# Turning a tile on VectorE and the DMA engines in place of TensorE, in a linear-attention retrieval kernel

## Chip, cores and metric

The kernel runs on one core of a Trainium2 chip. The metric is the device time of one execution in microseconds (us).

## What is computed

The reference is a layer norm followed by two branches that are added to the input. Cut to what matters (x has 8 x 256 rows of 512, G = 8 heads of size 128 are used):

```python
xn  = layernorm(x)
q   = xn @ Wq[used heads].T + bq             # 2048 x 1024
s   = elu(q) + 1
ret = (s @ M) / (s . z + 1e-6)               # per head of 128
out = x + repeat(ret, 4) @ Wo.T + xn @ (w * w_scale) + b
```

## The kernel before, in words

Rows are worked on in T = 16 tiles of 128. A weight matrix P = M . Wo (summed over the four repeats) is made once (`product_P`, eight heads), so that for a tile t the kernel needs q = x W (`product_q`, two halves of 512 columns), the dense branch (`product_dense`), s, the denominators, a = s / den (`make_a`), and a . P (`product_attn`). Every product is done in three passes of `float32r` data (hi.hi, hi.lo, lo.hi; lines 680 to 682), each a 128 x 128 weight load and a matmul of 512 columns: 24 matmuls for q, 12 for dense, 24 for attn.

`product_attn` needs a with the head dimension on the partitions. TensorE turns it: `transpose_a` (line 755) is eight 128 x 128 transposes a tile, into two PSUM banks `aT_ps`. ScalarE copies these to `aT_hi` (`copy_aT_hi`, line 388) and VectorE writes the remainder `aT_lo` (`split_aT_lo`, line 566); both are double buffered by t % 2.

The order on each engine is written out by hand, with semaphores between engines. After a head (tiles 0 to 6 of q and dense, the eight `product_P`), one loop runs t = 7 to 15 (LEAD = 7). In iteration t TensorE does `product_q(t)`, `product_dense(t)`, the mean of t+2, `product_attn(t-7)` and `transpose_a(t-5)`. VectorE does the split of tile t-6, `add_bias` (534), `moments` of t+2 (465 to 473), `make_s` (541), `split_xT_lo` (503), `add_dense` (557), `denominator(t-4)` (546 to 553) and `add_attn(t-7)` (573). ScalarE does the copy of tile t-6, the exponentials (367, 369), `copy_xT_hi` (344), `copy_mean` (329) and `make_a(t-4)` (380, eight instructions). GpSimd does `times_z` (261), `add_b` (268), `rstd_of` (224) and `center` (230). A tail then runs `product_attn` of tiles 9 to 15, with the transposes of 11 to 15 between.

SP issues all loads and stores in one order: in the loop `load_x` (162), `load_xT` (167) and the store of an old tile (210, 213). The repeated adds of Wo are issued from GpSimd (250). s sits in a ring `sbuf_s` of SRING = 7 tiles; a is made in place there. PSUM's eight banks are `q_ps` (2), `dense_ps`, `aT_ps` (2), `attn_ps` (2) and `mean_ps`; in the head q also borrows the `attn_ps` and `aT_ps` banks.

Of the kernel before, what the change touches and what calls it, by code (L numbers as in the profile page):

```python
# [5 lines left out]
F32 = mybir.dt.float32  # L6
F32R = mybir.dt.float32r
BF16 = mybir.dt.bfloat16
I8 = mybir.dt.int8
# [9 lines left out]
def retrieval_and_dense(nc, x_d, xT_d, WqT_d, bq_d, WoT_d, MT_d, z_d, w_d, wscale_d, b_d, out_d):  # L19
# [12 lines left out]
    SRING = 7  # L32
    XRING = 4
    HRING = 4
    BEHIND = 4
    assert P == D and HID == 512 and HALF == 512 and R == 4 and T == 16 and G == 8 and K == 4

    with ExitStack() as ctx:
# [41 lines left out]
        w_i8 = w_words[:].bitcast(I8)  # L80
# [13 lines left out]
        def q_bank(t, h):  # L94
            return ([q_ps, attn_ps, aT_ps][t % 3] if t < LEAD else q_ps)[h]
# [48 lines left out]
        aT_filled = sem("aT_filled")  # L144
# [8 lines left out]
        def halves(h):  # L153
            return slice(h * HALF, (h + 1) * HALF)

# [4 lines left out]
        def _(sp):  # L160
# [17 lines left out]

            load_x(0)
# [10 lines left out]
            sp.dma_start(w_words[:], w_d).then_inc(w_in, 16)  # L190
# [12 lines left out]
            for t in range(5, T):  # L203
                if t >= FIRST_LENT:
                    sp.wait_ge(P_filled, t - FIRST_LENT + 1)
                load_x(t)
                load_xT(t)
                if t >= 10:
                    sp.wait_ge(attn_added, t - 9)
                    sp.dma_start(out_d[t - 10], x[:, t - 10, :]).then_inc(stored, 16)  # L210
            for t in range(T - 10, T - 1):
                sp.wait_ge(attn_added, t + 1)
                sp.dma_start(out_d[t], x[:, t, :]).then_inc(stored, 16)
# [7 lines left out]
        def _(pool):  # L221
# [83 lines left out]
            center(7)  # L305
            add_b(0)
# [9 lines left out]
            for t in range(T - BEHIND, T):  # L316
                times_z(t, 0)
                times_z(t, 1)
                add_b(t - BEHIND + 2)
            for t in range(T - 2, T):  # L320
                add_b(t)

        @block.scalar
        def _(act):
# [58 lines left out]
            def copy_aT_hi(t):  # L383
                for h in range(2):
                    act.wait_ge(aT_filled, 2 * t + h + 1)
                    if t >= 2:
                        act.wait_ge(attn_filled, t - 1)
                    nc.scalar.activation(aT_hi[:, t % 2, h * GH:(h + 1) * GH, :].rearrange("p g r -> p (g r)"),  # L388
                                         aT_ps[h][:], ACT.Copy).then_inc(aT_hi_ready, 1)
# [54 lines left out]
            copy_mean(8)  # L444
            for t in range(LEAD, T):
# [12 lines left out]

        @block.vector
        def _(dve):  # L460
# [76 lines left out]
            def make_s(t, h):  # L537
                dve.wait_ge(exp_ready, 2 * t + h + 1)
                if h == 0 and t >= SRING:
                    dve.wait_ge(aT_filled, 2 * (t - SRING) + 2)  # L540
                nc.vector.scalar_tensor_tensor(sbuf_s[:, t % SRING, halves(h)], q_bank(t, h)[:], 0.0,  # L541
                                               ebuf[:, halves(h)], ALU.max, ALU.add).then_inc(s_ready, 1)
# [16 lines left out]

            def split_aT_lo(t):  # L560
                for h in range(2):
                    dve.wait_ge(aT_hi_ready, 2 * t + h + 1)
                    if t >= 2:
                        dve.wait_ge(attn_filled, t - 1)
                    gs = slice(h * GH, (h + 1) * GH)
                    nc.vector.tensor_tensor(aT_lo[:, t % 2, gs, :].rearrange("p g r -> p (g r)"), aT_ps[h][:],  # L566
                                            aT_hi[:, t % 2, gs, :].rearrange("p g r -> p (g r)").bitcast(F32),
                                            ALU.subtract).then_inc(aT_lo_ready, 1)
# [56 lines left out]
            denominator(1)  # L625
            make_s(4, 0)
# [9 lines left out]
            split_P_lo(1)  # L636
            add_dense(5)
# [4 lines left out]
            split_P_lo(3)  # L642
            split_xT_lo(7)
# [7 lines left out]
            split_P_lo(7)  # L651
            for t in range(LEAD, T):
# [12 lines left out]
            for t in range(T - LEAD, T - 1):  # L665
                split_aT_lo(t + 1)
                if t + 3 < T:
                    denominator(t + 3)
                add_attn(t)
# [8 lines left out]
        def _(pe):  # L678
# [67 lines left out]
            def transpose_a(t):  # L746
                pe.wait_ge(a_ready, t + 1)
                for h in range(2):
                    if t == 0:
                        pe.wait_ge(s_ready, 11 + h)  # L750
                    else:
                        pe.wait_ge(aT_lo_ready, 2 * t - 1 + h)
                    for i in range(GH):
                        g = h * GH + i
                        last = nc.tensor.transpose(aT_ps[h][:, i * P:(i + 1) * P],  # L755
                                                   sbuf_s[:, t % SRING, g * D:(g + 1) * D], ident[:])
                    last.then_inc(aT_filled, 1)

# [14 lines left out]
            for i in range(4):  # L773
                nc.tensor.matmul(aT_ps[i % 2][:], warm_r[:, 0:P], warm_r, start=True, stop=True)
# [65 lines left out]
            transpose_a(0)  # L840
# [3 lines left out]
            transpose_a(1)  # L844
            spread_mean(8)
            for t in range(LEAD, T):
                product_q(t, 0)
                product_q(t, 1)
                product_dense(t)
                if t + 2 < T:  # L850
                    spread_mean(t + 2)
                product_attn(t - LEAD)
                transpose_a(t - LEAD + 2)
            for t in range(T - LEAD, T - 1):
                product_attn(t)
                if t + 2 < T:
                    transpose_a(t + 2)
# [43 lines left out]
```

## Time and profile before

| | |
|---|---|
| median of 3 runs | 260.64 us (260.42 to 262.46) |
| profiled execution, its own time | 262.28 us |
| its span in the trace | 260.5 us |
| TensorE busy, share of the span | 251.3 us, 96% |
| VectorE busy | 154.8 us, 59% |
| ScalarE busy | 121.2 us, 47% |
| GpSimd busy | 103.2 us, 40% |
| mean granted TensorE clock | 0.993 |

Busy time is that in which an engine had an instruction running. A matmul is recorded with its whole passage through the array, so two that follow each other overlap in the records; what one costs the engine is the distance between two starts. The span is what the trace covers; the profiled execution's own time is 1.8 us longer.

### The profile page before, as it was taken

The numbers are of one execution on the slowest core, as the hardware profiler recorded it, in microseconds if no ns is written. First come the engines' busy times: TensorE is split into PE (matmuls) and PEld (weight loads), VectorE is DVE, ScalarE is ACT, GpSimd is POOL, SyncE is SP. The second block draws the span as 40 slices with busy tenths as digits, with TensorE's granted clock in tenths as the row PEclk, the third lists the DMA queues.
The fourth block names the chain that finished last, engine by engine and source line by source line (L and its number), as shares of the span: only waits on it lengthen the run. The fifth ranks groups of instructions, "written<-read, shape, count | busy, mean of one in ns | idle before, by whom it ended". The sixth has DMA issues, their size and how long they took to land.

```text
span 260.5 us, 3387 instructions
## 1 busy us (share of the span) xinstructions
PE 251.3 (96%) x1156; PEld 202.3 (78%) x1156; DVE 154.8 (59%) x262; ACT 121.2 (47%) x276; POOL 103.2 (40%) x96
## 2 busy tenths in 40 slices
PE   7799999899998999999999999999999999999996
PEld 4467777687775888888888888888888888888885
DVE  4558997985677745657384645657364345555321
ACT  2454545666439544534455444534445345555100
POOL 1565665671301770514426070514405055563000
PEclk9799999999999999999999999999999999999999
DMA  6999999996420003030301203010101001111111
GB/s 217 410 401 413 342 216 216 213 209 133 136 81 0 4 0 121 0 123 0 110 13 37 86 0 121 3 40 0 40 3 40 1 1 44 40 40 40 45 50 69
DMA packets 9808, 26.42 MB, mean 101 GB/s; under 512 B 1088, under 2 KB 1344, under 8 KB 8640
## 3 DMA queue, kind: packets, MB, share of 16 engines
q1 hardware_dynamic: 8928, 19.93, 20.9%
q0 software_dynamic: 864, 6.29, 12.0%
q8 instruction: 9, 0.15, 0.2%
q14 instruction: 7, 0.06, 0.1%
HBM read 22.02 MB, written 4.19 MB: 101 GB/s over the span
## 4 chain that ended last, share of the span: by engine, by line
PE 85%; DVE 7%; ACT 2%; DMA 2%; issue 2%; SPq 0%; DVEq 0%
PE attn_ps L682 11%; PE attn_ps L680 11%; PE attn_ps L681 11%; PE q_ps L680 8%; PE q_ps L682 8%; PE q_ps L681 8%; PE aT_ps L755 5%; PE dense_ps L680 5%; PE dense_ps L682 5%; PE dense_ps L681 5%; PE attn_ps L743 2%; DMA s<-in_WqT 2%; DVE wd_lo L520 1%; DVE q_ps L534 1%; DVE stats L465 1%
## 5 line engine op out<-in xcount | busy, mean ns | idle before, releaser
L261 POOL TENSOR_TENSOR e_and_sz<-s,z_b 128x512 f32<-128x512 f32 x32 | 41.8, 1324 | 32.7 <-DVE den L546 32.7
L380 ACT ACTIVATE s<-s,rden 128x128 f32<-128x128 f32 x128 | 39.2, 389 | 30.3 <-DVE rden L553 30.3
L680 PE MATMUL attn_ps<-P_hi,aT_hi 128*128 128x512 f32 (+1 forms) x128 | 50.2, 393 | 0.0
L682 PE MATMUL attn_ps<-P_hi,aT_lo 128*128 128x512 f32 (+1 forms) x128 | 49.2, 385 | 0.0
L681 PE MATMUL attn_ps<-P_lo,aT_hi 128*128 128x512 f32 (+1 forms) x128 | 49.0, 382 | 0.0
L573 DVE TENSOR_TENSOR x<-attn_ps,x 128x512 f32<-128x512 f32 x15 | 10.4, 691 | 46.4 <-PE attn_ps L682 46.4
L680 PE MATMUL q_ps<-WqT_hi,xT_hi 128*128 128x512 f32 x88 | 36.0, 409 | 0.6 <-DVE s L541 0.6
L682 PE MATMUL q_ps<-WqT_hi,xT_lo 128*128 128x512 f32 x88 | 34.4, 391 | 0.0
L681 PE MATMUL q_ps<-WqT_lo,xT_hi 128*128 128x512 f32 x88 | 34.3, 390 | 0.0
L230 POOL TENSOR_TENSOR xT<-xT,mean_b 128x512 f32<-128x512 f32 x14 | 19.4, 1383 | 33.1 <-ACT mean_b L329 33.1
L224 POOL TENSOR_TENSOR rstd<-vareps,neg_half 128x1 f32<-128x1 f32 x16 | 10.0, 626 | 54.8 <-DVE vareps L473 54.8
L534 DVE SCALAR_TENSOR_TENSOR q_ps<-q_ps,rstd,bq_b 128x512 f32<-128x512 f32 x24 | 18.1, 758 | 21.5 <-PE q_ps L682 21.5
L367 ACT ACTIVATE e_and_sz<-q_ps 128x512 f32<-128x512 f32 x24 | 14.3, 597 | 33.8 <-DVE q_ps L534 33.8
L680 PEld LDWEIGHTS attn_ps<-P_hi,aT_hi 128*128 128x128 f32 x128 | 24.1, 188 | 4.9
L682 PEld LDWEIGHTS attn_ps<-P_hi,aT_lo 128*128 128x128 f32 x128 | 24.0, 188 | 4.9
L681 PEld LDWEIGHTS attn_ps<-P_lo,aT_hi 128*128 128x128 f32 x128 | 24.1, 188 | 4.4
L680 PE MATMUL dense_ps<-wd_hi,xT_hi 128*128 128x512 f32 x64 | 25.7, 401 | 0.9 <-DVE x L557 0.9
L388 ACT ACTIVATE aT_hi<-aT_ps 128x512 fp32r<-128x512 f32 x32 | 17.4, 596 | 17.1 <-PE aT_ps L755 17.1
L682 PE MATMUL dense_ps<-wd_hi,xT_lo 128*128 128x512 f32 x64 | 25.0, 390 | 0.0
L681 PE MATMUL dense_ps<-wd_lo,xT_hi 128*128 128x512 f32 x64 | 24.9, 389 | 0.0
L566 DVE TENSOR_TENSOR aT_lo<-aT_ps,aT_hi 128x512 fp32r<-128x512 f32 x32 | 20.6, 686 | 5.2 <-ACT aT_hi L388 5.2
L369 ACT ACTIVATE e_and_sz<-e_and_sz 128x512 f32<-128x512 f32 x32 | 20.2, 633 | 1.0
(93 smaller groups left out, 408.3 us busy)
## 6 DMA issues: line engine op xcount, KB each, us to landing
x<-in_WoT POOLq DMA_DIRECT2D x6, 1024.0 KB, 9.5
x<-in_x SPq DMA_DIRECT2D x16, 256.0 KB, 3.5
xT<-in_xT SPq DMA_DIRECT2D x16, 256.0 KB, 3.9
out<-x SPq DMA_DIRECT2D x15, 256.0 KB, 2.0
x<-in_WoT SPq DMA_DIRECT2D x2, 1024.0 KB, 14.7
s<-in_WqT SPq DMA_DIRECT2D x3, 512.0 KB, 7.3
s<-in_w_scale SPq DMA_DIRECT2D x1, 1024.0 KB, 10.3
s<-in_WqT SPq DMA_DIRECT2D x2, 256.0 KB, 4.3
```

What stands on the lines that cost most here:

```text
L230: nc.gpsimd.tensor_tensor(xT[:, t % XRING, :, :], xT[:, t % XRING, :, :], mean_b[:, t % 2, :].unsqueeze(1).to_broadcast([P, K, P]), ALU.su ...
L261: nc.gpsimd.tensor_tensor(szbuf[:, halves(h)], sbuf_s[:, t % SRING, halves(h)], z_b[:, halves(h)], ALU.mult).then_inc(sz_ready, 1)
L367: nc.scalar.activation(e, q_bank(t, h)[:], ACT.Relu, scale=-1.0).then_inc(qneg_ready, 1)
L369: nc.scalar.activation(e, e, ACT.Exp, scale=-1.0).then_inc(exp_ready, 1)
L380: last = nc.scalar.activation(a_g, a_g, ACT.Copy, scale=rden[:, t % 2, g:g + 1])
L388: nc.scalar.activation(aT_hi[:, t % 2, h * GH:(h + 1) * GH, :].rearrange("p g r -> p (g r)"), aT_ps[h][:], ACT.Copy).then_inc(aT_hi_ready, 1)
L534: nc.vector.scalar_tensor_tensor(q_bank(t, h)[:], q_bank(t, h)[:], rstd[:, t:t + 1], bq_b[:, halves(h)], ALU.mult, ALU.add).then_inc(q_bia ...
L566: nc.vector.tensor_tensor(aT_lo[:, t % 2, gs, :].rearrange("p g r -> p (g r)"), aT_ps[h][:], aT_hi[:, t % 2, gs, :].rearrange("p g r -> p ...
L680: nc.tensor.matmul(out, x_hi, w_hi, start=start, stop=False)
L681: nc.tensor.matmul(out, x_hi, w_lo, start=False, stop=False)
L682: return nc.tensor.matmul(out, x_lo, w_hi, start=False, stop=stop)
L755: last = nc.tensor.transpose(aT_ps[h][:, i * P:(i + 1) * P], sbuf_s[:, t % SRING, g * D:(g + 1) * D], ident[:])
```

## The change

`transpose_a` and the `aT_ps` banks go. In their place VectorE transposes the 32 x 32 blocks of a tile in place in one instruction of 128 x 1024 (`turn_blocks`), and 16 transfers from SBUF to SBUF put block (i, j) of every head at place (j, i) (`spread_blocks`, issued by SP). Each transfer has 32 partitions, and on each of them eight runs of 32 elements (128 bytes): 256 runs, 32 KB. They land in a buffer `aT` for even tiles and in the memory of `MT` for odd ones (free once all eight `product_P` are done). `copy_aT_hi` and `split_aT_lo` now read SBUF. For tiles 12 to 15 SP issues 12 of the 16 transfers and ScalarE the other four (`spread_last_blocks`). BEHIND goes from 4 to 3, so a(t) is made one iteration earlier; SRING goes from 7 to 6; `w_words` shares the memory of `aT`. The two free PSUM banks become a second pair for q, so that `product_q(t)` waits for `make_s(t-2)` in place of t-1.

```diff
-    SRING = 7
+    SRING = 6
-    BEHIND = 4
+    BEHIND = 3
-        q_ps = [bank("q0_ps"), bank("q1_ps")]
-        aT_ps = [bank("aT0_ps"), bank("aT1_ps")]
+        q_ps = [bank(f"q{i}_ps") for i in range(4)]
# SP
+            def spread_blocks(t):
+                sp.wait_ge(a_turned, t + 1)
+                if t == 1:
+                    sp.wait_ge(P_filled, G)
+                elif t >= 2:
+                    sp.wait_ge(aT_lo_ready, 2 * t - 2)
+                a = sbuf_s[:, t % SRING, :].rearrange("p (g d) -> p g d", g=G)
+                for i in range(4 if t < T - BEHIND - 1 else 3):
+                    for j in range(4):
+                        sp.dma_start(aT_place(t)[j * 32:(j + 1) * 32, :, i * 32:(i + 1) * 32],
+                                     a[i * 32:(i + 1) * 32, :, j * 32:(j + 1) * 32]).then_inc(aT_in[t % 2], 16)
+            spread_blocks(0)
+            for t in range(FIRST_LENT, LEAD + 3):
+                sp.wait_ge(P_filled, t - FIRST_LENT + 1)
+                load_x(t)
+                load_xT(t)
+            spread_blocks(1)
+            spread_blocks(2)
+            for t in range(LEAD, T):
+                if t + 3 < T:
+                    sp.wait_ge(P_filled, t + 3 - FIRST_LENT + 1)
+                    load_x(t + 3)
+                    load_xT(t + 3)
+                spread_blocks(t - BEHIND - 1)
+                if t - LEAD >= 1:
+                    store(t - LEAD - 1)
+            for t in range(T - BEHIND - 1, T):
+                spread_blocks(t)
+                store(t - BEHIND - 1)
# GpSimd, head: times_z(3, 0), times_z(3, 1) after center(7)
# ScalarE
             def copy_aT_hi(t):
+                act.wait_ge(aT_in[t % 2], aT_landed(t))
-                    act.wait_ge(aT_filled, 2 * t + h + 1)
+            def spread_last_blocks(t):     # 4 transfers (i = 3) of tiles 12 to 15
+                act.wait_ge(a_turned, t + 1)
+                act.wait_ge(aT_lo_ready, 2 * t - 2)
             for t in range(LEAD, T):
-                copy_aT_hi(t - LEAD + 1)
                 exp_of(t, 0)
                 if t + 1 < T:
                     copy_xT_hi(t + 1)
                 exp_of(t, 1)
+                copy_aT_hi(t - LEAD + 1)
             for t in range(T - LEAD + 1, T):
                 copy_aT_hi(t)
-                if t + 2 < T:
-                    make_a(t + 2)
+                if t + BEHIND < T:
+                    make_a(t + BEHIND)
+                if T - BEHIND - 3 <= t < T - 2:
+                    spread_last_blocks(t + 2)
# VectorE; head: turn_blocks(0), (1), (2) and denominator(3) are added
+            def turn_blocks(t):
+                dve.wait_ge(a_ready, t + 1)
+                nc.vector.transpose(sbuf_s[:, t % SRING, :], sbuf_s[:, t % SRING, :]).then_inc(a_turned, 1)
             for t in range(LEAD, T):
-                split_aT_lo(t - LEAD + 1)
                 add_bias(t, 0)
                 ...
                 add_bias(t, 1)
+                turn_blocks(t - BEHIND - 1)
                 make_s(t, 0)
                 ...
                 make_s(t, 1)
+                split_aT_lo(t - LEAD + 1)
                 add_dense(t)
                 denominator(t - BEHIND)
+                if t == T - 1:
+                    denominator(T - BEHIND)
                 add_attn(t - LEAD)
             for t in range(T - LEAD, T - 1):
                 split_aT_lo(t + 1)
+                if t + BEHIND < T:
+                    turn_blocks(t + BEHIND)
+                if t + BEHIND + 2 < T:
+                    denominator(t + BEHIND + 2)
                 add_attn(t)
# TensorE: transpose_a and its calls are removed
-                pe.wait_ge(s_ready, 2 * (t - 3 if t < LEAD else t - 1) + h + 1)
+                pe.wait_ge(s_ready, 2 * (t - 3 if t < LEAD else t - 2) + h + 1)
```

## Rows read from the trace of the kernel before

**Rows 1.** The page: span, busy time of TensorE, shares of the chain that ended last.

```profile
span 260.5 us, 3387 instructions
...
PE 251.3 (96%) x1156; PEld 202.3 (78%) x1156; DVE 154.8 (59%) x262; ACT 121.2 (47%) x276; POOL 103.2 (40%) x96
...
PE 85%; DVE 7%; ACT 2%; DMA 2%; issue 2%; SPq 0%; DVEq 0%
```

**Rows 2.** Busy time in stretches: us, then each engine, granted clock, DMA share, GB/s.

```profile
112.00:124.00 12.00, 12.00 (x58) 9.95 (x57) 8.26 (x15) 4.94 (x10) 3.07 (x3) 1.00 0.21 68
220.00:240.00 20.00, 20.00 (x105) 16.84 (x104) 10.95 (x19) 11.20 (x33) 11.47 (x10) 1.00 0.10 39
```

**Rows 3.** The chain that ended last, in order of time: start, us, what.

```profile
97.09 0.88 PE aT_ps L755 x8
...
97.96 0.24 PE q_ps L680
98.20 0.23 PE q_ps L681
...
126.38 0.87 PE aT_ps L755 x8
...
141.06 0.87 PE aT_ps L755 x8
...
220.42 0.87 PE aT_ps L755 x8
221.29 0.23 PE attn_ps L680
...
226.52 0.23 PE attn_ps L682
226.75 0.87 PE aT_ps L755 x8
```

**Rows 4.** VectorE's timeline in the head: start, us, what, idle before.

```profile
62.48 0.76 DVE L534 SCALAR_TENSOR_TENSOR aT_ps<-aT_ps,rstd,bq_b 128x512 f32<-128x512 f32 x1 [1.97 <-PE aT_ps L682]
69.84 0.75 DVE L557 SCALAR_TENSOR_TENSOR x<-dense_ps,rstd,x 128x512 f32<-128x512 f32 x1 [1.56 <-PE dense_ps L682]
79.19 1.28 DVE L566 TENSOR_TENSOR aT_lo<-aT_ps,aT_hi 128x512 fp32r<-128x512 f32 x2
```

**Rows 5.** Groups of instructions by line: busy us, mean ns of one, idle before.

```profile
L546 DVE TENSOR_REDUCE den<-e_and_sz 128x8 f32<-128x1024 f32 x16 | 19.3, 1209 | 0.0
L503 DVE TENSOR_TENSOR xT_lo<-xT,xT_hi 128x512 fp32r<-128x512 f32 x15 | 14.2, 944 | 3.9 <-ACT xT_hi L344 3.8
L520 DVE TENSOR_TENSOR wd_lo<-s,wd_hi 128x1024 fp32r<-128x1024 f32 x2 | 3.4, 1762 | 0.0
L573 DVE TENSOR_TENSOR x<-attn_ps,x 128x512 f32<-128x512 f32 x15 | 10.4, 691 | 46.4 <-PE attn_ps L682 46.4
```

**Rows 6.** Timeline of SP's queue: start, us of the issue, what.

```profile
97.84 0.35 SPq L210 DMA_DIRECT2D out<-x  x1
98.23 0.43 SPq L162 DMA_DIRECT2D x<-in_x  x1
98.71 0.46 SPq L167 DMA_DIRECT2D xT<-in_xT  x1
```

**Rows 7.** Busy time in stretches that hold one 256 KB store, and half of one.

```profile
186.00:187.80 1.80, 1.80 (x9) 1.48 (x8) 1.29 (x2) 0.59 (x2) 0.00 (x0) 1.00 0.39 146
256.20:257.00 0.80, 0.80 (x9) 0.80 (x8) 0.00 (x0) 0.00 (x0) 0.00 (x0) 1.00 0.48 164
```

**Rows 8.** DMA issues of the page: count, KB each, median us to landing.

```profile
out<-x SPq DMA_DIRECT2D x15, 256.0 KB, 2.0
```

**Rows 9.** Timelines of ScalarE and VectorE in the tail.

```profile
220.89 1.09 ACT L388 ACTIVATE aT_hi<-aT_ps 128x512 fp32r<-128x512 f32 x2 [0.39 <-PE aT_ps L755]
224.41 2.45 ACT L380 ACTIVATE s<-s,rden 128x128 f32<-128x128 f32 x8 [2.44 <-DVE rden L553]
234.22 1.29 DVE L566 TENSOR_TENSOR aT_lo<-aT_ps,aT_hi 128x512 fp32r<-128x512 f32 x2 [0.38 <-ACT aT_hi L388]
252.18 0.69 DVE L573 TENSOR_TENSOR x<-attn_ps,x 128x512 f32<-128x512 f32 x1 [3.97 <-PE attn_ps L682]
```

More of the change, by code:

```diff
@@ L94, in q_bank @@
         def q_bank(t, h):
-            return ([q_ps, attn_ps, aT_ps][t % 3] if t < LEAD else q_ps)[h]
+            if t < LEAD and t % 3 == 1:
+                return attn_ps[h]
+            return q_ps[2 * (t % 3 == 2 if t < LEAD else t % 2) + h]
         def last_attn_ps(c):
@@ L143, in retrieval_and_dense @@
         dense_added = sem("dense_added")
-        aT_filled = sem("aT_filled")
+        a_turned = sem("a_turned")
+        aT_in = [sem(f"aT_in{i}") for i in range(2)]
         aT_hi_ready = sem("aT_hi_ready")
@@ L202, in _ @@
             sp.dma_start(b_b[:], b_d.unsqueeze(0).to_broadcast([P, HID])).then_inc(b_in, 16)
-            for t in range(5, T):
-                if t >= FIRST_LENT:
-                    sp.wait_ge(P_filled, t - FIRST_LENT + 1)
+            for t in range(5, FIRST_LENT):
                 load_x(t)
                 load_xT(t)
[L208 to L213, printed above, removed]
+            spread_blocks(0)
[16 more added lines that the diff above has]
+                store(t - BEHIND - 1)
+            for t in range(T - BEHIND - 1, T - 1):
+                store(t)
             for c in range(2):
@@ L305, in _ @@
             center(7)
+            times_z(3, 0)
+            times_z(3, 1)
             add_b(0)
@@ L318, in _ @@
                 times_z(t, 1)
-                add_b(t - BEHIND + 2)
-            for t in range(T - 2, T):
+                add_b(t - 3)
+            for t in range(T - 3, T):
                 add_b(t)
@@ L383, in copy_aT_hi @@
             def copy_aT_hi(t):
+                act.wait_ge(aT_in[t % 2], aT_landed(t))
+                if t >= 2:
+                    act.wait_ge(attn_filled, t - 1)
                 for h in range(2):
-                    act.wait_ge(aT_filled, 2 * t + h + 1)
[L386 to L389, printed above, removed]
+                    gs = slice(h * GH, (h + 1) * GH)
+                    nc.scalar.activation(aT_hi[:, t % 2, gs, :], aT_place(t)[:, gs, :], ACT.Copy).then_inc(aT_hi_ready, 1)
+            def spread_last_blocks(t):
+                act.wait_ge(a_turned, t + 1)
+                act.wait_ge(aT_lo_ready, 2 * t - 2)
+                a = sbuf_s[:, t % SRING, :].rearrange("p (g d) -> p g d", g=G)
+                for j in range(4):
+                    act.dma_start(aT_place(t)[j * 32:(j + 1) * 32, :, 96:], a[96:, :, j * 32:(j + 1) * 32]
+                                  ).then_inc(aT_in[t % 2], 16)
             copy_wq_hi(0, 0)
@@ L444, in _ @@
             copy_mean(8)
+            make_a(3)
             for t in range(LEAD, T):
-                copy_aT_hi(t - LEAD + 1)
                 exp_of(t, 0)
@@ L539, in make_s @@
                 if h == 0 and t >= SRING:
-                    dve.wait_ge(aT_filled, 2 * (t - SRING) + 2)
+                    dve.wait_ge(aT_in[(t - SRING) % 2], aT_landed(t - SRING))
                 nc.vector.scalar_tensor_tensor(sbuf_s[:, t % SRING, halves(h)], q_bank(t, h)[:], 0.0,
@@ L642, in _ @@
             split_P_lo(3)
+            denominator(3)
             split_xT_lo(7)
@@ L744, in product_P @@
                                  ).then_inc(P_filled, 1)
[L746 to L757, printed above, removed]
             def product_attn(t):
@@ L773, in _ @@
             for i in range(4):
-                nc.tensor.matmul(aT_ps[i % 2][:], warm_r[:, 0:P], warm_r, start=True, stop=True)
+                nc.tensor.matmul(q_ps[2 + i % 2][:], warm_r[:, 0:P], warm_r, start=True, stop=True)
             pe.wait_ge(consts_set, 3)
```

29 lines of the change are left out of this document (16 added, 13 removed).

## The prediction

> **What bounds the kernel now.** I read the page first. TensorE is busy for 96% of the span and holds 85% of the chain that ended last [rows 1]. A busy TensorE need not be full, so next come the stretches. In the loop and in the tail it is busy without a gap and at the full clock, while VectorE has 3.7 us free in 12 and the DMA engines are 0.1 to 0.2 busy [rows 2]. Then the chain in order of time: in the loop it never leaves TensorE, and its links follow each other at 0.23 us a matmul. From one group of eight transposes to the next are 141.06 - 126.38 = 14.68 us in the loop and 226.75 - 220.42 = 6.33 us in the tail [rows 3]. So from about 83 us on, where the loop begins, the end is set by how much TensorE is given to do, and anything else decides only when it delivers later than TensorE asks.
>
> **What the change takes away.** One `transpose_a` holds TensorE for 0.87 us [rows 3]. Two lie in the head, nine in the loop (tiles 2 to 10), five in the tail (11 to 15). The 14 behind 83 us give 14 x 0.87 = 12.2 us, if TensorE is still fed. A tile then costs 14.68 - 0.87 = 13.8 us in the loop and 5.46 in the tail.
>
> The two in the head I count at nothing. There `product_P` alternates with the P splits on two banks, and VectorE paces it. The change adds to VectorE three turns and `denominator(3)` (1.21 + 0.17 + 0.20, some 1.6 us), while the 1.28 us split of tile 0 [rows 4] stays among the P splits. The turns of tiles 0 and 1 fit in waits of 1.97 and 1.56 us [rows 4]; `denominator(3)` stands before `split_P_lo(4)` with only short waits to absorb it. Against 2 x 0.87 = 1.7 us gained stand about 1.6 us of VectorE. The bounds are 1.7 us of gain and 1.5 us of loss; I take 0.
>
> **What it adds to VectorE.** The block transpose of 128 x 1024 is not in this trace. Nearest are other instructions of VectorE that read 1024 elements: a reduction at 1.21 us, and a subtraction at 1.76 [rows 5]. I take 1.2, since both have one pass over 1024 elements and the reduction has one input as the transpose has; an upper bound is 2 x 1.21 = 2.4 us. In an iteration the order is bias (q half 0 is full at 2.7 us after the iteration's start), moments 1.1, bias (q half 1 at 5.5), turn, make_s, xT split, make_s, aT split, add_dense, denominator. By the durations of the trace the xT split that the next iteration needs at 13.8 us ends near 8.8, so the turn has 5 us of cover, even at 2.4 us. Behind the turn also queue `add_dense`, due 19.2 us after the start and done near 11.6, and the aT split, due at 22 and done near 10.8. VectorE's sum a tile is 10.1 to 11.3 of 13.8 us. Cost: 0. What the trace cannot say is whether SBUF as source makes the aT copies and splits longer; the 0.69 us of an addition from PSUM against a mean of 0.94 of the xT splits [rows 5], which were longer while GpSimd and DMAs were busy, says at most 0.25 us each, which is under the same cover.
>
> Here a rule speaks against the change. TensorE's transposes cost it 0.87 / 8 = 0.11 us each in the stream [rows 3]. The Trainium skill (VectorE: DVE Perf Modes, section Rules for kernel authors) says to transpose 128 x 128 on TensorE where PSUM will do as destination, and keeps VectorE for 32 x 32. By that rule the detour costs more in total, which is true in busy time here (1.2 us and 16 transfers for 0.87 us); it would lose only if the other queues were on the path.
>
> **What it adds to SP.** This is the term that decides. Each tile costs 16 issues. Now an issue of 128 runs takes 0.35 us after a pause and 0.43 to 0.46 behind another, and back to back the starts are 0.48 us apart [rows 6]. Call this distance c. The new transfers have 256 runs of 128 bytes. If issue time does not depend on the runs, c is 0.48; if all of it is proportional to them, c is 0.05 + 2 x 0.43 = 0.91. There is no row for 256 runs. I take 0.50, near the row, because the issue rows hardly differ between transfers and the wait for a preceding one accounts for most of what does.
>
> In the loop SP has 16c + 3 x 0.48 = 9.4 us a tile against 13.8. The period is passed at c = 0.77. Latency is covered as well: `spread_blocks(t-4)` starts in iteration t once the aT split of t-6 is done, near 10.8 us, ends near 19 and lands 2 us later (a store takes 2.0 [rows 8]); `copy_aT_hi` wants it 7.5 us into iteration t+2, thus at 35. Queued behind it on SP are one store, which nobody awaits before the end, and the loads for t+4, which are wanted a whole iteration later. BEHIND = 3 costs nothing for the same reason: `make_a(t-3)` has the denominators at 13.2 and the turn asks 6 us later. The three spreads at the loop's start are the tightest: tile 1 must wait for the last `product_P` (about 82 us), is issued by 90.5, lands at 92.5, and its copy is wanted at about 91 with slack of 10 us to the product. Cost 0.
>
> **The tail** is where 16 transfers meet 5.46 us. SP issues 12 (ScalarE four, 2 us of its 5.5, in the gaps between a 1.09 us copy and a 2.45 us `make_a` [rows 9]). SP has 12c + 0.48 = 6.5 us a tile at c = 0.50, so it falls behind by 1 us a tile for tiles 12 to 15. Its chain: the last iteration starts at 83.4 + 8 x 13.8 = 193.6. There GpSimd and VectorE need until 17.1 us to have the denominators of tile 13, then come `add_attn(8)` 0.7, the split of tile 10 1.3 and the turn of tile 12 1.2, so spread 12 starts at 20.3, thus at 213.9. Four spreads take 48c + 3 x 0.48. Then landing 2.0, half a copy 0.55, half a split 0.65, and from the start of the last product to the end of the span 260.5 - 252.2 = 8.3 us [rows 1, 9]. Sum: 213.9 + 1.4 + 11.5 + 48c = 226.8 + 48c. With c = 0.50 it is 250.8, with 0.48 it is 249.8, both above what TensorE alone would give, 260.5 - 12.2 = 248.3. So the tail gives back 2.5 of the 12.2 us.
>
> **The DMA engines.** A store of 128 packets of 2 KB holds the 16 engines for 0.39 x 1.8 x 16 = 11.2 us, one of 128 packets of 1 KB for 0.48 x 0.8 x 16 = 6.1 us [rows 7]. The difference is 0.040 us a KB, and about 7 ns a packet are left. A packet of 128 bytes is then 12 ns by the straight line; it is at most the 43 ns of a 1 KB packet, if small packets cost a fixed price. An engine gets 256 of them a tile: 3 to 11 us. I take 3, since the line went through both rows. In the loop even 11 + 2.1 of other traffic (three times 11.2 / 16) fit in 13.8; in the tail 11 do not fit in 5.46.
>
> **The sum.** 260.5 - 12.2 + 2.5 = 250.8 of span, 9.7 less than before. The profiled execution's own time was 262.28, the median 260.64; taken from the median this gives 250.9, which I round to 251.
>
> **The rivals.**
> (1) The issue grows with the runs, to c of 0.58 to 0.69. The tail's formula gives 254.6 to 259.9 of span, thus 254.7 to 260.1. For it: twice as many descriptors must be made by something. Against: 0.35 us after a pause holds the fixed work of an issue as well, so the part for each run is less than 0.35 / 128.
> (2) SP is the bound, slower. From c = 0.69 on the whole chain of spreads decides: 82.3 (last `product_P`) + 11 x 16c + 48c + 6 pairs of loads and 11 stores (11.0) + 11.5 = 104.8 + 224c; it passes 260.5 at 0.695, and gives 284 at c = 0.80 and 309 at 0.91. ScalarE would then wait for `aT_in`, and with it the exponentials, `make_s` and in the end `product_q`.
> (3) Packets of 128 bytes cost as much as 1 KB ones. The tail's pace is then 11 us a tile: 213.9 + 44 + 2 + 11.5 = 271 us. For it: nothing under 1 KB of data stands in the trace. Against: the straight line through two sizes, which leaves 7 ns a packet. The Trainium skill (DMA: Bandwidth & Descriptors, section Specifications) says that below 512 bytes the engines read, modify and write; that would be on this side. The same page (section Bandwidth) holds that transfers between SBUF and SBUF are spared the price of small descriptors, and no run here shows either yet.
> (4) The change does not get its gain for another reason: a wait in the head or a late `x` load. `load_x(10)` stands behind spreads 1 and 2, ends near 101 us and is wanted at 100.7. Some 1 to 3 us, 252 to 254.
>
> **How the numbers follow.** Forecast with (4): 0.53, thus 251. Rival (1) 0.18, half of it below 258.0. Rivals (2) and (3) 0.16 and 0.10, to which I add 0.03 for slower by several small terms. Low end: 248.3 of span with the head's 1.7 gained is 246.6. High end: to leave out no more than 0.2, it takes in rival (3) at 271. A measurement of this kernel cannot tell less than about 1% (2.6 us) from no change. Faster by over 1%: 0.53 + 0.09 = 0.62, and less 0.02 for a head worse than its bound, 0.60. Within 1%: 0.11. Slower: 0.29.
>
> **What would show it.** Right: SP's issues of `spread_blocks` 0.48 to 0.52 us apart; 60 matmuls a tile at 13.8 us; no wait of TensorE in the loop; waits of TensorE for the aT split, under 3 us in total, in the last three or four tiles; a turn at 1.2 us; VectorE's busy time up by some 19 us. Wrong: SP's issues over 0.6 us; ScalarE waiting for the transfers in the loop; a DMA share over 0.5 in the loop; TensorE's gaps before the loop begins, which would show that the head was mis-sized.

## The result, and the profile after

The changed kernel takes 267.51 us (median of 4 runs, 266.14 to 268.63) against 261.55 for the kernel before on the same chip (4 runs, 260.42 to 262.5): ratio 1.0213, 95% interval 1.0145 to 1.028. It is slower by 2.1%, with 1.5 to 2.8% as the interval. The four executions of the changed kernel have spans of 264.3 to 266.8 us, so a span below is compared to about 1 us, and a time inside one trace more closely. The profiled execution took 268.2 us, with a span of 266.4, where the forecast had 250.8. So 15.6 us are to be explained.

The page of the changed kernel: span, busy times, the chain that ended last by engine, then its largest lines; it answers to [rows 1].

```profile
span 266.4 us, 3393 instructions
...
PE 242.3 (91%) x1028; PEld 190.7 (72%) x1028; DVE 179.7 (67%) x278; ACT 120.2 (45%) x276; POOL 105.0 (39%) x96
...
PE 53%; SPq 24%; DVE 12%; issue 4%; DMA 4%; ACT 3%; DVEq 0%
SPq L197 22%; PE q_ps L742 7%; PE q_ps L744 7%; PE q_ps L743 7%; PE attn_ps L742 6%; PE attn_ps L744 6%; PE attn_ps L743 6%; PE dense_ps L742 4%; PE dense_ps L743 4%; PE dense_ps L744 4%; DMA s<-in_WqT 2%; PE attn_ps L805 2%; DVE stats L515 1%; DVE aT_lo L620 1%; DMA x<-in_x 1%
```

TensorE's 85% of the chain have become 53%, and SP's queue, which held 0%, now has 24%, nearly all of it at line 197, the transfers of `spread_blocks`. Next, the waits of TensorE: total, times, longest.

```profile
PE attn_ps L742 <- DVE aT_lo L620: 9.2, 5, 3.0
PE mean_ps L752 <- DVE meanvar L519: 4.0, 3, 3.3
PE dense_ps L742 <- DVE x L607: 3.1, 1, 3.1
```

Each names VectorE, but the cause behind each is another one. For the first, SP's queue shows it: start, us of a whole group of issues, and what. It answers to [rows 6].

```profile
84.22 10.95 SPq L197 DMA_DIRECT2D MT<-s  x16
95.27 10.73 SPq L197 DMA_DIRECT2D aT<-s  x16
106.05 0.60 SPq L171 DMA_DIRECT2D x<-in_x  x1
106.69 0.43 SPq L176 DMA_DIRECT2D xT<-in_xT  x1
...
220.65 7.81 SPq L197 DMA_DIRECT2D aT<-s  x12
228.50 0.60 SPq L202 DMA_DIRECT2D out<-x  x1
229.19 7.87 SPq L197 DMA_DIRECT2D MT<-s  x12
237.11 0.61 SPq L202 DMA_DIRECT2D out<-x  x1
237.82 7.94 SPq L197 DMA_DIRECT2D aT<-s  x12
245.80 0.60 SPq L202 DMA_DIRECT2D out<-x  x1
246.50 8.56 SPq L197 DMA_DIRECT2D MT<-s  x12
```

In the tail one tile follows another at 229.19 - 220.65 = 8.5 us and 246.50 - 237.82 = 8.7, with no pause between groups, while TensorE has 5.46 us of work for each. Twelve issues take 7.81 us, 0.65 each. That is what paces the waits for `aT_lo`. The first two of the five (1.36 and 1.23 us) have a share of ScalarE's: its copy of the tile began right behind its own four issues (219.90 to 222.86, and 228.25 to 230.86). From the third on (1.75, 2.96, 1.85) the copy waited for the transfers themselves. Where the first wait ends, VectorE's split also took 1.74 us beside GpSimd's work, for 0.69 as a rule.

The second wait is at the start of the loop. VectorE's timeline (start, us, what, idle before), and the stretches around it (as in [rows 2]):

```profile
103.06 0.75 DVE L584 SCALAR_TENSOR_TENSOR q_ps<-q_ps,rstd,bq_b 128x512 f32<-128x512 f32 x1
109.15 0.69 DVE L515 BATCH_NORM_STATS2 stats<-x 128x6 f32<-128x512 f32 x1 [5.34 <-DMA x<-in_x]
```

```profile
106.00:108.00 2.00, 0.82 (x4) 0.36 (x2) 0.00 (x0) 0.73 (x2) 0.00 (x1) 1.00 0.54 60
108.00:110.00 2.00, 0.00 (x0) 0.00 (x0) 0.81 (x2) 0.00 (x0) 0.00 (x0) 0.91 0.90 282
110.00:112.00 2.00, 1.88 (x5) 1.59 (x6) 1.97 (x5) 1.02 (x2) 0.55 (x1) 0.50 0.31 50
112.00:114.00 2.00, 2.00 (x8) 1.52 (x8) 2.00 (x5) 1.41 (x4) 0.51 (x1) 0.73 0.31 50
...
118.00:202.00 84.00, 84.00 (x373) 69.20 (x373) 60.83 (x95) 42.13 (x103) 35.43 (x31) 1.00 0.41 92
```

`load_x(10)` is issued at 106.05, behind 32 transfers. `moments(10)` waits for it 5.34 us, the mean product waits for the moments, and TensorE stands for 3.3 us. Then its granted clock is 0.50 (the 1.2 GHz level) for 2 us and 0.73 for 2 more, which costs another 1.0 + 0.54 us: 4.8 in all. The last row is the rest of the loop but its last iteration: TensorE is busy without a gap at the full clock, as forecast.

The third is in the head, in VectorE's timeline:

```profile
44.03 1.21 DVE L596 TENSOR_REDUCE den<-e_and_sz 128x8 f32<-128x1024 f32 x1
45.27 2.04 DVE L599 TENSOR_SCALAR den_e<-den 128x8 f32<-128x8 f32 x1
...
47.46 0.70 DVE L607 SCALAR_TENSOR_TENSOR x<-dense_ps,rstd,x 128x512 f32<-128x512 f32 x1
```

The addition of 128 x 8 takes 2.04 us where it usually takes 0.17, and `add_dense(2)`, for which TensorE waits, stands behind it. GpSimd's timeline has three instructions back to back over the same time:

```profile
43.97 1.57 POOL L267 TENSOR_TENSOR xT<-xT,mean_b 128x512 f32<-128x512 f32 x1
45.22 0.82 POOL L261 TENSOR_TENSOR rstd<-vareps,neg_half 128x1 f32<-128x1 f32 x1
45.76 1.52 POOL L298 TENSOR_TENSOR e_and_sz<-s,z_b 128x512 f32<-128x512 f32 x1
```

The addition ends at 47.31, as the last of them does (47.28). TensorE's granted clock falls behind this stop too, as it did at tile 10 (the third number from the end is the granted clock):

```profile
48.00:50.00 2.00, 1.78 (x4) 1.49 (x5) 2.00 (x5) 2.00 (x7) 0.99 (x2) 0.55 1.15 242
50.00:52.00 2.00, 2.00 (x7) 1.53 (x6) 0.62 (x2) 0.03 (x1) 1.22 (x1) 0.59 0.92 177
```

Those are another 0.9 + 0.8 us of TensorE's time. How much of this reaches the loop's start, the experiments show.

### The profile page after: what moved, and what is told of

Same layout as the page of the kernel before. It is cut to its first block, busy times and chain, and to the rows that moved or that the text cites. A ratio compares the mean times of both kernels' runs of the same rounds, so it can differ in the third digit from the quotient of the medians.

```text
span 266.4 us, 3393 instructions
## 1 busy us (share of the span) xinstructions
PE 242.3 (91%) x1028; PEld 190.7 (72%) x1028; DVE 179.7 (67%) x278; ACT 120.2 (45%) x276; POOL 105.0 (39%) x96
## 3 DMA queue, kind: packets, MB, share of 16 engines
q0 software_dynamic: 864, 6.29, 11.5%
## 4 chain that ended last, share of the span: by engine, by line
PE 53%; SPq 24%; DVE 12%; issue 4%; DMA 4%; ACT 3%; DVEq 0%
SPq L197 22%; PE q_ps L742 7%; PE q_ps L744 7%; PE q_ps L743 7%; PE attn_ps L742 6%; PE attn_ps L744 6%; PE attn_ps L743 6%; PE dense_ps L742 4%; PE dense_ps L743 4%; PE dense_ps L744 4%; DMA s<-in_WqT 2%; PE attn_ps L805 2%; DVE stats L515 1%; DVE aT_lo L620 1%; DMA x<-in_x 1%
## 5 line engine op out<-in xcount | busy, mean ns | idle before, releaser
L742 PE MATMUL q_ps<-WqT_hi,xT_hi 128*128 128x512 f32 x104 | 41.8, 402 | 0.9 <-DVE s L591 0.6
L744 PE MATMUL q_ps<-WqT_hi,xT_lo 128*128 128x512 f32 x104 | 40.6, 390 | 0.0
L743 PE MATMUL q_ps<-WqT_lo,xT_hi 128*128 128x512 f32 x104 | 40.5, 390 | 0.0
L584 DVE SCALAR_TENSOR_TENSOR q_ps<-q_ps,rstd,bq_b 128x512 f32<-128x512 f32 x28 | 21.1, 756 | 25.1 <-PE q_ps L744 25.0
L742 PEld LDWEIGHTS attn_ps<-P_hi,aT_hi 128*128 128x128 f32 x128 | 24.9, 194 | 16.3 <-issue 8.9
L406 ACT ACTIVATE e_and_sz<-q_ps 128x512 f32<-128x512 f32 x28 | 16.6, 594 | 21.8 <-DVE q_ps L584 21.8
L744 PE MATMUL dense_ps<-wd_hi,xT_lo 128*128 128x512 f32 x64 | 25.4, 397 | 0.0
L620 DVE TENSOR_TENSOR aT_lo<-MT,aT_hi 128x512 fp32r<-128x512 f32 x16 | 15.8, 1027 | 13.5 <-ACT aT_hi L428 13.5
L591 DVE SCALAR_TENSOR_TENSOR s<-q_ps,e_and_sz 128x512 f32<-128x512 f32 x28 | 18.7, 674 | 7.6 <-DMA MT<-s 4.3
L742 PEld LDWEIGHTS q_ps<-WqT_hi,xT_hi 128*128 128x128 f32 x104 | 19.5, 188 | 6.0 <-issue 1.2
L743 PEld LDWEIGHTS q_ps<-WqT_lo,xT_hi 128*128 128x128 f32 x104 | 19.5, 188 | 4.4 <-issue 0.5
L744 PEld LDWEIGHTS q_ps<-WqT_hi,xT_lo 128*128 128x128 f32 x104 | 19.5, 188 | 4.2
```

Of the source, the lines that this page charges most:

```text
L406: nc.scalar.activation(e, q_bank(t, h)[:], ACT.Relu, scale=-1.0).then_inc(qneg_ready, 1)
L584: nc.vector.scalar_tensor_tensor(q_bank(t, h)[:], q_bank(t, h)[:], rstd[:, t:t + 1], bq_b[:, halves(h)], ALU.mult, ALU.add).then_inc(q_bia ...
L620: nc.vector.tensor_tensor(aT_lo[:, t % 2, gs, :], aT_place(t)[:, gs, :], aT_hi[:, t % 2, gs, :].bitcast(F32), ALU.subtract).then_inc(aT_lo ...
L742: nc.tensor.matmul(out, x_hi, w_hi, start=start, stop=False)
L743: nc.tensor.matmul(out, x_hi, w_lo, start=False, stop=False)
L744: return nc.tensor.matmul(out, x_lo, w_hi, start=False, stop=stop)
```

## The experiments

All edits are to the changed kernel unless another is named, and `...` marks lines left out. Ratios are to the kernel before, timed on the same chip. "Spread 12" is the start of the first group of 12 transfers in SP's queue, where the tail's chain begins (220.65 in the changed kernel); "loop start" is the first product of q for tile 7 (83.05 before, 84.66 after).

**Is it the queue's order that stops the loop?** `load_x(10)` and `load_x(11)` go ahead of the spreads of tiles 1 and 2, later loads one iteration earlier.

```diff
-            for t in range(FIRST_LENT, LEAD + 3):
+            for t in range(FIRST_LENT, LEAD + 5):
...
-                if t + 3 < T:
+                if LEAD < t and t + 4 < T:
...
```

> The changed kernel with the loads of tiles 10 and 11 issued by SP ahead of the spreads of tiles 1 and 2, and later loads one iteration earlier. Theory A (SP's order and its issue time make the loss): VectorE's wait of 5.3 us for tile 10's x goes, and TensorE's gap of 3.1 us near 107 us and the half clock behind it with it; the last iteration starts 4 to 5 us earlier, so do the spreads of the tail, span 261 to 262.5. Theory B (the spreads are late at the tail for their own sake, SP busy without pause from 84 us on): the start of spread 12 stays near 220 us and the span at 265 to 266.

Measured: 264.52 us (4 runs, 262.2 and 262.7, 266.4 and 266.6: too far apart for a ratio). The profiled one is of the faster pair, span 260.9, 5.5 less; so the size is read inside the trace. The stretches of this kernel, where the changed one stood still:

```profile
106.00:108.00 2.00, 2.00 (x11) 1.61 (x10) 1.23 (x3) 1.97 (x5) 0.17 (x1) 1.00 0.30 49
108.00:110.00 2.00, 2.00 (x10) 1.63 (x9) 2.00 (x3) 0.72 (x3) 1.20 (x1) 1.00 0.30 49
```

Spread 12 comes at 215.39, 5.3 earlier, of which 0.4 was there at the loop start. So the queue's order cost 4.9 us between the loop's start and spread 12, which is the stop and the slow stretch behind it (4.8). The tail's pace is unchanged (215.39, 223.92, 232.58, 241.26).

**Is it `denominator(3)` that makes the head late?**

```diff
-            denominator(3)
             ...
             split_P_lo(7)
+            denominator(3)
```

> The changed kernel with denominator(3) behind the last P split on VectorE instead of ahead of the fifth. Theory A (the head's 1.8 us are those 1.6 us of VectorE in the chain of P): the loop starts 1.5 us earlier, near 83.4 us; the end gains up to 1.5 us, or nothing if the stall for tile 10's x swallows it. Theory B (the head is late because of something else, an odd long instruction near 45 us in that trace): the loop's start moves by less than 0.5 us apart from what that instruction costs.

Measured: 266.75 us (265.15 to 268.95), ratio 1.016 (1.0079 to 1.0241), not told apart from the changed kernel. The profiled execution is the fastest of the four, span 263.4. There the loop starts 3.8 us earlier (80.90), but most of that is not the edit's. The held-up addition fell elsewhere in this trace, in `denominator(1)`, TensorE's wait for `add_dense` is 1.2 instead of 3.1, and its clock stays at 1.00 behind it. The loop starts of the traces, sorted by which addition was held up and by where `denominator(3)` stands, part the two (the others are from experiments below):

| held up | `denominator(3)` as changed | `denominator(3)` late |
|---|---|---|
| `denominator(0)`, ahead of `add_dense(2)` | 84.66; 84.29 (loads first), 84.17 (half the runs), 84.26 (tail by TensorE), 84.77 (128 partitions) | 84.13 (three edits) |
| `denominator(1)` | 81.90 (four transfers) | 80.90 (this kernel), 80.91 (three edits, two inputs) |
| none | 82.88 (one run) | |

So the move is worth 0.0 to 0.6 us in the first row and 1.0 in the second, and the hold-up ahead of `add_dense(2)` 2.3 to 3.2. These are single traces, and the last row shows that about 1 us between two of them needs no such cause. The stop for tile 10's x is still there (TensorE stands for 3.6 us): spread 12 at 217.37, the end 3.0 earlier.

**Does the issue grow with the runs?** Only heads 0 to 3 are moved (ScalarE's four transfers likewise): half the runs and bytes. The turned values of the other heads are left out.

```diff
-  sp.dma_start(aT_place(t)[j * 32:(j + 1) * 32, :, i * 32:(i + 1) * 32],
-               a[i * 32:(i + 1) * 32, :, j * 32:(j + 1) * 32])
+  sp.dma_start(aT_place(t)[j * 32:(j + 1) * 32, 0:4, i * 32:(i + 1) * 32],
+               a[i * 32:(i + 1) * 32, 0:4, j * 32:(j + 1) * 32])
```

> The transfers carry only heads 0 to 3 (the turned values of heads 4 to 7 are left out): 16 transfers of 128 runs in place of 256, in the same two-dimensional form. If the issue grows with the runs, it falls from 0.61 to about 0.43 us and the starts to 0.48 us apart, the tail's SP chain from 8.6 to 6.3 us a tile, and the span to 252 to 255. If the two-dimensional form makes the issue long, it stays at 0.61 us and the span at 265 to 266.

Measured: 268.19 us (266.03 to 268.65), ratio 1.0193 (1.0121 to 1.0264), span 266.8. SP's queue:

```profile
107.41 10.24 SPq L197 DMA_DIRECT2D MT<-s  x16
...
221.88 7.69 SPq L197 DMA_DIRECT2D aT<-s  x12
```

10.24 us for 16 against 10.39 with twice the runs: 0.01 us of an issue hangs on 128 runs. Rival (1) had the size of the issue right and its reason wrong.

**What is the change worth when issues cost nothing?** From tile 2 on only the four transfers with i = j are made (one of them by ScalarE for tiles 12 to 15, and what the copies wait for is lowered to match); the other twelve blocks are left out.

```diff
-                    for j in range(4):
+                    for j in range(4) if t < 2 else range(i, i + 1):
```

> From tile 2 on only the four diagonal transfers of a tile are issued (the other twelve blocks are left out), each with its 256 runs. SP is off the path. Theory A: the removed transposes then show their worth, the tail runs at 5.5 us a tile; the head's 1.8 us and what spread 1 does to the first iteration stay, span 250 to 252. Theory B (something besides SP's issue holds TensorE, as VectorE's extra work or slower reads from SBUF): span 256 or more.

Measured: 248.13 us (247.48 to 252.18), ratio 0.9437 (0.9372 to 0.9502), span 246.6, 13.9 less than before. TensorE has no wait for `aT_lo` and none for the x of tile 10. The chain's shares, and SP's queue:

```profile
PE 82%; DVE 10%; ACT 3%; issue 2%; DMA 2%; SPq 1%; DVEq 0%
```

```profile
107.15 2.55 SPq L197 DMA_DIRECT2D aT<-s  x4
121.02 2.55 SPq L197 DMA_DIRECT2D MT<-s  x4
134.78 2.55 SPq L197 DMA_DIRECT2D aT<-s  x4
148.53 2.55 SPq L197 DMA_DIRECT2D MT<-s  x4
```

The starts follow each other at 13.75 us, the period that the prediction worked out. Of the 13.9 us, 1.15 are an earlier loop start (81.90) and 12.75 lie behind it, for 12.2 forecast there. So with the issues out of the way TensorE's gain comes in full.

**The tail alone.** Tiles 12 to 15 go by TensorE as before, into the second pair of q banks; the other twelve stay as changed.

```diff
+        aT_ps = q_ps[2:]
+        ON_PE = T - BEHIND - 1
-            for t in range(T - BEHIND - 1, T):
-                spread_blocks(t)
-                store(t - BEHIND - 1)
...
+                if ON_PE <= t + 2 < T:
+                    transpose_a(t + 2)
```

> The changed kernel, but tiles 12 to 15 are turned by TensorE as before (into the second pair of q banks, free by then). Theory A (in the tail SP's issue is the pace): the tail goes from 8.6 to 5.5 + 0.9 us a tile, and the gaps of TensorE after 230 us go. By the starts of the changed kernel: loop 84.9, plus 5.4 us of the stall for tile 10's x, plus 9 x 13.8, 6 x 5.46, 4 x 0.87 and 8.3 at the end, 259 us of span. Theory B (TensorE waits in the tail for slower copies and splits whatever turns the tiles): no more than 2 us gained, 264 or more.

Measured: 260.55 us (258.86 to 261.69), ratio 0.9895 (0.9817 to 0.9973), span 259.4. The waits for `aT_lo` are gone, the other two stay:

```profile
PE mean_ps L760 <- DVE meanvar L523: 4.6, 3, 3.8
PE dense_ps L750 <- DVE x L611: 3.2, 1, 3.2
```

The span is 7.0 us shorter, although TensorE has 4 x 0.87 = 3.5 us more to do: the queueing in the tail (SP's, and ScalarE's part of it) cost three times what the change saved there.

**All three edits together.** The loads first, `denominator(3)` later, the tail by TensorE.

> Three edits together: the loads of tiles 10 and 11 ahead of the first spreads, denominator(3) behind the P splits, tiles 12 to 15 turned by TensorE. If the three places are all there is: 83.4 + 9 x 13.8 + 6 x 5.46 + 4 x 0.87 + 8.3 = 252.2 us of span, faster than before by 3%. If an instruction of VectorE again sits blocked for 2 to 3 us in the head, 254 to 256.

Measured: 254.44 us (6 runs, 251.42 to 255.65), ratio 0.9648 (0.9578 to 0.9718), span 252.5. Of the three waits one is left, 3.0 us for `add_dense`, behind an addition of 1.99 us at 45.17.

**What makes the issue long?** Two forms of the 16 transfers, 32 KB each as before, ScalarE's four likewise; data lands in wrong places, so a . P is made of elements in another order. First 32 partitions with one run of 1 KB:

```diff
-  aT_place(t)[j * 32:(j + 1) * 32, :, i * 32:(i + 1) * 32], a[i * 32:(i + 1) * 32, :, j * 32:(j + 1) * 32]
+  aT_place(t)[j * 32:(j + 1) * 32, 2 * i:2 * i + 2, :],     a[i * 32:(i + 1) * 32, 2 * j:2 * j + 2, :]
```

> The same 16 transfers of 32 KB a tile from 32 to 32 partitions, but each partition's 1 KB in one run instead of eight (the blocks go to wrong places; the turning is left out). If the second dimension of the pattern makes the issue long, it falls from 0.61 to 0.43 us. If it is the 32 partitions, or a source in SBUF, it stays at 0.61.

Measured: one run, 264.62 us, span 262.8. The issues of its SP queue:

```profile
104.95 10.02 SPq L197 DMA_DIRECT2D MT<-s  x16
115.01 0.59 SPq L171 DMA_DIRECT2D x<-in_x  x1
115.65 0.43 SPq L176 DMA_DIRECT2D xT<-in_xT  x1
```

Then all 128 partitions with one run of 256 bytes, the partitions of a load but between SBUF and SBUF:

```diff
+  aT_place(t)[:, 2 * i + j // 2, 64 * (j % 2):64 * (j % 2) + 64], a[:, 2 * i + j // 2, 64 * (j % 2):64 * (j % 2) + 64]
```

> The 16 transfers of a tile still go from SBUF to SBUF with 32 KB each, but every one has 128 partitions with one run of 256 bytes (the values land in wrong places; the turning is left out). If the 32 partitions make the issue long, it falls from 0.58 to 0.43 us. If a source in SBUF does, it stays near 0.6, and then every transfer inside SBUF costs SP 0.17 us more than one from HBM.

Measured: one run, 268.19 us, span 266.4.

```profile
107.00 10.13 SPq L197 DMA_DIRECT2D MT<-s  x16
117.18 0.59 SPq L171 DMA_DIRECT2D x<-in_x  x1
117.82 0.43 SPq L176 DMA_DIRECT2D xT<-in_xT  x1
```

Neither runs nor partitions matter: 10.02, 10.13, 10.24 and 10.39 us for 16, with 32 to 256 runs. What all four share and the loads (0.43) do not is that both ends are in SBUF. They are also smaller (16 or 32 KB). Size made no difference between 16 and 32 KB here, nor in the head of the kernel before between loads of 256 and 1024 KB (0.43 each), but no small transfer from HBM was run. So the two ends are what is left by exclusion, not what was shown. The first load or store behind such a group also takes 0.58 to 0.61, which an explanation by the two ends alone does not cover; what the queue does there stays open.

**Does the head gain from TensorE too?** The three edits, and tiles 0 and 1 turned by TensorE as before, with their turns, spreads 0 and 1 and the places in SP's queue taken out.

```diff
-            return t >= ON_PE
+            return t < 2 or t >= ON_PE
```

> As the kernel with the three edits, and tiles 0 and 1 turned by TensorE too (no transfer before tile 2). Two transposes cost 1.7 us in the head, but VectorE loses two turns there, and make_s(7) no longer waits for tile 1 to land. If those waits touch TensorE, 251 to 253 of span, as good as or better than with three edits; if not, 1 to 2 us more than there, 253 to 254.

Measured: 255.43 us (6 runs, 252.32 to 258.46), ratio 0.9671 (0.9601 to 0.9741), span 250.5. By the intervals, no difference from the three edits: turning the first two tiles costs or gives nothing that can be told.

**Is it the form of the blocked addition?** It is written with two inputs, in the kernel with the three edits, in that of the head by TensorE, and in the kernel before.

```diff
-                nc.vector.tensor_scalar_add(den_e[:], den[:], DEN_EPS)
+                nc.vector.scalar_tensor_tensor(den_e[:], den[:], DEN_EPS, den[:], ALU.add, ALU.max)
```

> The kernel with the three edits, and the small addition of the denominators (128x8, one input in SBUF) written with two inputs, (den + eps) max den, the same values. In all traces of changed kernels but one, this instruction once took 2.0 to 3.5 us in place of 0.17 in the head, beside GpSimd's work, and TensorE waited and fell to half its clock. Theory A (the one-input form is kept out for as long as GpSimd has work back to back): the two-input form never takes over 1.5 us, the span falls by 2 to 4 us to 249 to 250.5, and the runs scatter less. Theory B (any instruction of VectorE at that place is kept out): it takes 2 to 3 us as before and the span stays at 252 to 253.

> The kernel in which also tiles 0 and 1 are turned by TensorE, with the same small edit. Theory A: 2 to 3 us less than without it where the addition was kept out, 248 to 250 us of span, runs within 2 us instead of 6. Theory B: as without, 250 to 256.

> The kernel before, with the same small edit of the denominators. Its eleven runs so far lie at 260.3 to 264.9 us. Theory A: its slower runs are those in which the addition is kept out, so all runs come near 260.5 us. Theory B: no change, 260 to 265.

Measured: 253.59 us (6 runs, 251.15 to 256.44), ratio 0.9655 (0.959 to 0.9721); 253.23 (6 runs, 252.26 to 254.93), ratio 0.968 (0.9633 to 0.9728); the kernel before with it, 262.77 (12 runs), ratio 1.0012 (0.9972 to 1.0051). VectorE's timeline of the first of these:

```profile
54.13 3.67 DVE L603 SCALAR_TENSOR_TENSOR den_e<-den 128x8 f32<-128x8 f32 x1
```

The form is not the reason: this one was held up for 3.67 us, and that of the head by TensorE for 2.11.

**Take `add_dense` out from behind the addition.**

```diff
-            denominator(0)
             add_dense(2)
+            denominator(0)
```

> The changed kernel with add_dense(2) ahead of denominator(0) on VectorE. In its trace the small addition of denominator(0) sat for 2.04 us behind GpSimd's work and kept add_dense(2) from TensorE, which waited 3.1 us and then ran at half its clock for some 3 us. Theory A (that is part of the head's loss): the wait for add_dense in the head goes, the loop starts 2 to 4 us earlier, 262 to 264 us of span if it isn't swallowed by the stall for tile 10's x. Theory B (that stall and VectorE's chain of P set the loop's start anyway): within 1 us of 266.

Measured: 264.10 us (12 runs, 263.24 to 266.91), ratio 1.008 (1.0034 to 1.0126), span 265.1. The profiled execution is the slowest of the twelve. The wait for `add_dense` is gone, and the loop starts at 82.37, 2.3 us earlier. The held-up addition is now that of `denominator(1)` (55.35, 3.29 us), behind which TensorE does not wait. The stop for tile 10's x returns most of it: spread 12 is only 1.4 us earlier.

**All four edits together.**

> The kernel with the three edits and the same swap. Theory A: its profiled run goes from 252.5 to 249 to 250.5 us of span and its median from 254.4 to 251 to 252. Theory B: the addition is kept out at another place of the head instead (denominator(1), as in two other traces) and the median stays at 253 to 254.5.

Measured: 250.49 us (6 runs, 248.82 to 252.09), ratio 0.9523 (0.9462 to 0.9585), span 248.7, granted clock 1.0. The page's busy times and chain, and VectorE's timeline:

```profile
PE 238.6 (96%) x1060; PEld 191.0 (77%) x1060; DVE 178.3 (72%) x274; ACT 119.8 (48%) x276; POOL 104.7 (42%) x96
...
PE 86%; DVE 6%; ACT 2%; DMA 2%; issue 2%; SPq 0%; DVEq 0%
```

```profile
44.02 0.74 DVE L611 SCALAR_TENSOR_TENSOR x<-dense_ps,rstd,x 128x512 f32<-128x512 f32 x1
...
53.14 4.53 DVE L603 TENSOR_SCALAR den_e<-den 128x8 f32<-128x8 f32 x1
```

and TensorE's, a little later:

```profile
59.74 1.10 PE L813 MATMUL attn_ps<-x,MT 128*128 128x512 f32 x2 [0.84 <-DVE s L595]
```

The chain is TensorE's again, as it was before the change, and the loop starts at 80.36. This version beats both kernels, 4.8% under the kernel before. An addition is held up for 4.53 us; `make_s` stands behind it, and TensorE waits 0.84 us for that, instead of 3 us and a slow stretch. Whether the kernel before would gain from the same swap was not run; its waits for `add_dense` are only 0.9 us in all.

## Why the prediction was wrong, by its steps

**The tail, the largest part.** The step that failed is "I take 0.50": the terms 48c and 1.4 gave four spreads 25.4 us. From 220.65 to 255.06 they took 34.4, 9.0 more: 48 x 0.15 = 7.2 because the issues start 0.65 apart, 0.8 because each of the three stores between takes up 0.74 instead of 0.48, and 1.0 more, most of it in the last group (8.56). The row taken as nearest was of loads from HBM, and the text even named the only thing it doubted, the runs; what made the issue long was not them (10.02 us for 16 issues with 32 runs, 10.39 with 256). That it is the two ends in SBUF is left by exclusion. The mechanism and the formula were right, but for ScalarE, whose four issues took 2.6 to 3.0 us for 2 forecast and stood ahead of its copy. With c = 0.65 it gives 226.8 + 31.2 = 258.0, inside rival (1)'s span; the rest of the miss lies ahead of the tail.

**The loop's start, the second part.** Spread 12 began at 220.65 instead of 213.9, 6.75 later, of which 1.3 are the head's. (83.4 + 8 x 13.8 is 193.8 and not 193.6, so the sum should have said 214.1.) The step is the loop's "Cost 0" for SP and, in rival (4), "Some 1 to 3 us". The queue order was seen, with `load_x(10)` behind spreads 1 and 2, but its size rested on the same c: 32 issues at 0.65 take 21 us instead of 16, so that the load was issued at 106.05. Moving the load brought 4.9 us. That TensorE would come back at a lower clock (0.50 and 0.73 in the two stretches behind) after 3.3 us of standing was not in the sum; it is 1.5 of these 4.9.

**The head.** Taken as 0 within -1.7 to +1.5. The loop began at 84.66, 1.3 us later than the 83.4 used, and 1.6 later than in the kernel before (83.05), so just outside the bounds. And the step's reason, `denominator(3)` against two transposes, was the smaller part. By the table of loop starts `denominator(3)` cost 0 to 1 us (2.0 between the two kernels with `add_dense` moved, 82.37 and 80.36, the first of them at half the clock from 82 to 84). The hold-up of an addition ahead of `add_dense(2)`, which the prediction did not know, cost 2.3 to 3.2; against it stands what the head gained. The sum of the miss: 9.0 + 6.75 - 0.2 (the end behind the last spread, 11.3 instead of 11.5) = 15.6.

**What held.** TensorE's side: 13.75 us a tile in the kernel with four transfers, and 13.9 us of span gained there against 12.2 + 1.7 forecast as the most. That the two are equal is partly luck: 12.75 came behind the loop's start for 12.2, and 1.15 ahead of it for 1.7. The turn: 1.232 us (mean of 16) for 1.2 forecast. The landing of the transfers: 1.9 for 2.0. The small packets: between 219 and 221 us, 816 packets of 128 bytes took 30.3% of 16 engines' time, as the DMA view of that stretch has it:

```profile
DMA packets 816, 0.10 MB, mean 49 GB/s; under 512 B 816, under 2 KB 816, under 8 KB 816
...
q1 hardware_dynamic: 816, 0.10, 30.3%
```

0.303 x 2 us x 16 / 816 = 11.9 ns each, as the straight line said (12); rival (3) is out. (Its own price was read too low: 6.1 us over 128 packets is 48 ns and not 43. And its sum counts the landing twice, once in the 11.5.) Of the two sections of the Trainium skill set side by side in the prediction (DMA: Bandwidth & Descriptors), the trace agrees with Bandwidth, that transfers between SBUF and SBUF are spared the penalty of small descriptors, and not with Specifications' read-modify-write below 512 bytes, as far as time goes.

The splits became longer at the mean, 1.03 and 0.94 us a half (16 each, from `MT` and `aT`) for 0.69, which is up to 0.34 each and over the bound of 0.25. But SBUF as source is not enough for it: the median is 0.69 as before, the last two, with GpSimd done, took 1.30 us together, and single ones beside GpSimd's work up to 1.78. It stayed under cover in the loop; in the tail one such split ended TensorE's first wait. VectorE's busy time rose by 24.9 us for 19 forecast: 19.7 are the turns, the rest mostly these splits and the hold-up. The DMA share in the loop was 0.41. Rival (2), SP as the bound of the whole loop, did not come: 16c + 1.5 = 12 us is under 13.8, yet c = 0.65 is close to the 0.695 at which that chain alone would have reached the old span.

The range of 246.6 to 271.0 held the time only because it took in rival (3), whose mechanism was not the one at work. That is luck.

## What to carry to other kernels

Before moving work to the DMA queues, count the issues by the issuing engine, take the price of one from a row of the same kind of transfer (both ends in SBUF here: starts 0.65 us apart, not 0.48), and compare groups of them with the period of every stage, the shortest above all: 12 issues at 0.65 us do not fit in 5.5 us, though 16 fit in 13.8. A load that stands behind such a group is as late as the whole group; put it ahead. A mixed solution, with the detour where the period is long and the old way where it is short, and with the loads ahead of the groups and `denominator(3)` later, gained 3.5% where the whole change lost 2.1%; with `add_dense` moved too it gained 4.8%.

## What the hardware showed that was not expected

- An issue of a transfer of 16 or 32 KB between SBUF and SBUF by SP took 0.59 to 0.61 us at the median (starts 0.63 to 0.65 apart, single issues up to 2.0 us), with 32, 128 or 256 runs and 32 or 128 partitions, against 0.43 for loads of 256 KB and more from HBM. The first issue of the other kind behind them took 0.58 to 0.61 as well.
- An addition of 128 x 8 elements on VectorE, 0.17 us as a rule, took 2.0 to 4.5 us once in the head of each changed kernel but that with one run of 1 KB, and ended there within 0.04 us of the end of a 128 x 512 product of GpSimd; the form with two inputs did too (3.67 and 2.11 us). In the six kernels whose tail is turned by TensorE it took 1.25 to 1.27 us a second time, in the tail. Each time GpSimd had an instruction under way, or was issuing a transfer, as the addition began. In the two traces of the kernel before, with either form, none of the 32 additions began so: they fell in GpSimd's pauses, most of them 0.05 us ahead of its next instruction. But GpSimd at work is not enough: in the kernels with `denominator(3)` late, with the head by TensorE and with the three edits and two inputs, an addition at 45.3 to 45.5 began beside GpSimd's work by the records (which are rough for GpSimd) and took 0.17. What decides between the two is open. The Trainium skill (SBUF — State Buffer, section SBUF: two separate sides) holds that VectorE and GpSimd share a pair of ports as an exclusive lock, and names instructions with two SBUF inputs and the fast modes as those that need it. Ends that coincide agree with that; that the wait outlasts several of GpSimd's instructions, and not one, is what the traces add.
- After 3.3 us without work TensorE ran at a granted clock of 0.50 for 2 us and 0.73 for the next 2, having been at 1.00 before. In the same trace stops of 3.1 us (head: 0.55, then 0.59) and 3.0 us (tail, from 250: 0.50, then 0.75) were followed by the same, and stops of 1.2 to 1.8 us at 224 to 240 were not (1.00).
